# Local attention of a two-layer attention block on one Trainium2 core: elementwise products replaced by block matmuls with masks as contraction rows

## Chip, cores and metric

One core of a Trainium2 chip. The metric is device time in microseconds (us) of one execution; the page and the traces are of one profiled execution.

## What is computed

The input x has 16 images of 64 channels and 56 x 56 pixels, float32. Two residual layers follow each other:

```python
x = x + L0(_gn(x), ...)   # window attention: 7 x 7 windows, 16 channels a head
x = x + L1(_gn(x), w_out, b_out)
# L1, local attention, KSIZE 5, 8 heads of 8 channels:
patches = extract_patches(x)                        # 25 shifted copies, zero outside the image
p = patches.reshape(N, NHEADS, hdim, K2, H, W)
q = x.reshape(N, NHEADS, hdim, 1, H, W)
scores = (p * q).sum(axis=2, keepdims=True)
att = jax.nn.softmax(scores, axis=3)                # over the 25 shifts
out = (p * att).sum(axis=3).reshape(N, D, H, W)
out = jnp.einsum('ndhw,od->nohw', out, w_out) + b_out[None, :, None, None]
```

`_gn` normalises groups of two channels over the image. A pixel outside the image has score 0 and value 0, but it counts in the softmax's total.

## The kernel before, in words

Partitions hold two images by 64 channels; the 8 pairs of images are `BP`. There are three stages.

Stage 1, window attention (the functions up to L1162 on DVE, L1361 on PE): 64 units in a loop, each with four passes of scores (L1321), transposes (L1330) and weighing (L1346). It is the same in both kernels. After it, DVE and PE compute the second layer's group statistics; the last step of that is L1065.

Stage 2, local attention, L1186 to L1247 on DVE, L1419 to L1498 on PE. x1 is written to DRAM with a border of zeros (`widen_x1`, L583) and is read back in two layouts, one for scores and one for values. Then for each of the 8 heads j:

- Scores: 13 shifts of a half plane times 2 channel halves. A product of pixels and shifted pixels, 128 x 1568, is made on DVE for head 0 (L1194) and on POOL for the others (L799), with the square on ACT. PE adds the channels with the matrix `fold` (`sum_scores`, L1428 and L1432), and ACT copies the map twice, once mirrored (L965, L969).
- Softmax: DVE takes the maximum of 25 maps (L1203) and subtracts it (L1209), ACT takes exponentials (L988), PE adds the total (L1444 to L1461), DVE inverts it (L1227).
- Values: 25 shifts times 2 halves. ACT copies a weight map to PSUM (`place_weight`, L997), DVE multiplies it into shifted pixels (L1220), or POOL does (L810), and PE adds the products with the identity (`sum_values`, L1484), 16 matmuls of 32 x 32 tiles for each product. ACT copies the sum out (L1008), POOL scales it (L815), SP stores it in DRAM.

The order on all engines in stage 2 is written by a planner, `merge_orders` (L173), which simulates the steps with written costs. Tiles go round in rings of four (`ring`, `v_tiles`).

Stage 3: attention and x1 are loaded from DRAM, PE projects (L1507: 64 matmuls of 392 columns with 128 x 128 weights), DVE adds (L1255), SP stores.

## Time and profile before

| what | value |
|---|---|
| runs, median of 2 | 1743.34 us (1738.09 to 1748.59) |
| profiled execution, span from first to last instruction | 1743.6 us |
| PE busy | 1434.3 us, 82% |
| DVE busy | 1396.1 us, 80% |
| ACT busy | 1030.6 us, 59% |
| POOL busy | 1139.6 us, 65% |
| DMA | 152.35 MB, mean 87 GB/s |

The span and the median agree within 0.3 us, so a sum that is made in the profiled execution stands for the runs. Busy time is the union of an engine's instructions: where 16 matmuls run side by side in different tiles of the array, they count once. "PEld" are the weight loads, which lie beside the matmuls. "Idle before" is time that an engine spent without work ahead of a group, with what ended it.

### The profile page before, as it was taken

Reading aid. Unit: us, or ns where it says so; the run is one execution under the profiler, and the core shown is the slowest. Engines: PE = TensorE matmul, PEld = TensorE weight load, DVE = VectorE, ACT = ScalarE, POOL = GpSimd, SP = SyncE. Lnnn points to the kernel's source line nnn. Section 1 sums busy time; section 2 is a strip of 40 time slices with the busy share of each in tenths; the row PEclk is TensorE's granted clock in tenths of the full one; section 3 lists DMA queues with packets and bytes.
Section 4 is the critical chain, followed back from the end, with each engine's and each line's share of the span. In section 5 each row is a group of like instructions: output and inputs, shape, how many; then the busy total and the mean of one; then the engine's idle time right before and its main releaser. Section 6 shows DMA issues by size and latency. Waiting matters only on the chain.

```text
span 1743.6 us, 62829 instructions
## 1 busy us (share of the span) xinstructions
PE 1434.3 (82%) x26281; PEld 755.6 (43%) x26281; DVE 1396.1 (80%) x1964; ACT 1030.6 (59%) x1861; POOL 1139.6 (65%) x873
## 2 busy tenths in 40 slices
PE   4989999999999999974597888879797786966754
PEld 2656666666666666651132332323233232322332
DVE  4774777777777777778999999999989999995933
ACT  3554777777777777754564747667474766543300
POOL 5333555555555555530679999999999999985700
PEclk9775999999999999987699999999999999997978
DMA  8702011111104220215202324223232522126079
GB/s 330 301 11 52 18 34 39 28 46 24 50 17 100 21 55 18 55 33 141 52 20 59 98 52 122 52 73 91 58 79 51 122 52 71 39 67 244 22 309 388
DMA packets 106870, 152.35 MB, mean 87 GB/s; under 512 B 71362, under 2 KB 83650, under 8 KB 100034
## 3 DMA queue, kind: packets, MB, share of 16 engines
q1 hardware_dynamic: 106690, 149.67, 29.4%
q8 instruction: 147, 2.41, 0.6%
q14 instruction: 33, 0.27, 0.1%
HBM read 77.99 MB, written 65.20 MB: 82 GB/s over the span
## 4 chain that ended last, share of the span: by engine, by line
PE 44%; DVE 18%; POOL 16%; issue 13%; ACT 5%; SPq 1%; DMA 1%; DVEq 0%; POOLq 0%; ACTq 0%
POOL arena L799 11%; PE PS L1484 7%; PE PS L1321 7%; PE PS L1330 5%; PE PS L1346 5%; DVE arena L1111 4%; PE PS L1298 4%; POOL arena L810 4%; PE PS L1290 4%; DVE arena L1107 4%; PE PS L1507 3%; PE PS L1428 3%; PE PS L1309 2%; PE PS L1360 2%; ACT arena L988 2%
## 5 line engine op out<-in xcount | busy, mean ns | idle before, releaser
L1220 DVE TENSOR_TENSOR arena<-arena,PS 128x1568 f32<-128x1568 f32 x334 | 583.9, 1777 | 16.1 <-PE PS L1484 8.3
L799 POOL TENSOR_TENSOR arena<-arena 128x1568 f32<-128x1568 f32 x168 | 517.7, 3123 | 87.7 <-PE PS L1428 68.1
L765 POOL TENSOR_TENSOR arena<-arena,consts 128x196 f32<-128x196 f32 x512 | 294.3, 609 | 283.7 <-ACT arena L849 283.7
L1484 PE MATMUL PS<-arena,consts 32*32 32x392 f32 x12800 | 396.9, 512 | 78.3 <-DVE arena L1220 23.4
L997 ACT ACTIVATE PS<-arena 128x392 f32<-128x392 f32 x334 | 166.3, 501 | 255.8 <-DVE arena L1220 255.1
L1428 PE MATMUL PS<-arena,consts 128*32 128x392 f32 x1664 | 200.3, 554 | 83.2 <-POOL arena L799 42.1
L1107 DVE TENSOR_REDUCE arena<-PS 128x8 f32<-128x392 f32 x256 | 143.2, 559 | 144.7 <-PE PS L1321 143.2
L1484 PEld LDWEIGHTS PS<-arena,consts 32*32 32x32 f32 x12800 | 145.8, 104 | 246.0 <-issue 96.1
L874 ACT ACTIVATE arena<-PS 128x512 f32<-128x512 f32 x256 | 152.9, 597 | 161.0 <-PE PS L1330 157.2
L810 POOL TENSOR_TENSOR arena<-arena 128x1568 f32<-128x1568 f32 x66 | 202.7, 3081 | 29.4 <-ACT arena L937 20.7
L1330 PE MATMUL PS<-consts,arena 128*128 128x128 f32 x1024 | 177.9, 299 | 0.2
L1346 PE MATMUL PS<-arena 128*64 128x34 f32 x4096 | 176.8, 232 | 0.7 <-DVE arena L1124 0.7
L1321 PE MATMUL PS<-arena 64*64 64x196 f32 x2048 | 166.4, 397 | 1.8 <-POOL arena L765 1.1
L1346 PEld LDWEIGHTS PS<-arena 128*64 128x64 f32 x4096 | 147.5, 143 | 46.8 <-issue 46.0
L1111 DVE TENSOR_TENSOR arena<-PS,arena 128x392 f32<-128x392 f32 x256 | 145.4, 568 | 18.7
L867 ACT ACTIVATE arena<-arena 128x392 f32<-128x392 f32 x256 | 137.8, 538 | 33.1 <-DVE arena L1111 24.0
L772 POOL TENSOR_TENSOR arena<-arena 128x392 f32 (+1 forms) x64 | 78.4, 1225 | 109.3 <-DVE arena L1136 109.3
L1330 PEld LDWEIGHTS PS<-consts,arena 128*128 128x128 f32 x1024 | 113.9, 147 | 64.4 <-issue 52.2
L1428 PEld LDWEIGHTS PS<-arena,consts 128*32 128x32 f32 x1664 | 35.8, 112 | 219.7 <-issue 102.1
L928 ACT ACTIVATE arena<-arena,consts 128x504 f32<-128x504 f32 (+1 forms) x128 | 104.8, 856 | 14.6 <-DMA arena<-x_wide_dram 9.7
L862 ACT ACTIVATE arena<-PS 49x256 f32<-49x256 f32 x256 | 95.5, 373 | 24.6 <-PE PS L1309 23.1
L1203 DVE TENSOR_TENSOR PS<-arena,PS 128x392 f32<-128x392 f32 x192 | 108.1, 563 | 2.2
(109 smaller groups left out, 1724.2 us busy)
## 6 DMA issues: line engine op xcount, KB each, us to landing
arena<-x_wide_dram SPq DMA_DIRECT2D x32, 660.0 KB, 8.2
arena<-x_wide_dram SPq DMA_DIRECT2D x256, 67.5 KB, 2.0
x_wide_dram<-arena SPq DMA_DIRECT2D x12, 1125.0 KB
arena<-in_x_dram SPq DMA_DIRECT2D x8, 1568.0 KB, 14.5
x_wide_dram<-arena SPq DMA_DIRECT2D x64, 196.0 KB, 4.3
x_dram<-arena SPq DMA_DIRECT2D x8, 1568.0 KB, 7.5
attn_dram<-arena SPq DMA_DIRECT2D x256, 49.0 KB, 3.0
arena<-x_dram SPq DMA_DIRECT2D x8, 1568.0 KB, 19.0
```

The lines of the kernel that those rows point to most:

```text
L765: i = nc.gpsimd.tensor_tensor(k_bd[k][:, r], keys.unsqueeze(1).to_broadcast([P, HEADS_T, S]), head_mask.unsqueeze(2).to_broadcast([P, HEAD ...
L799: nc.gpsimd.tensor_tensor(tile, x_part, by, ALU.mult).then_inc(pool_tile, 1)
L810: nc.gpsimd.tensor_tensor(tile, *by, ALU.mult).then_inc(pool_tile, 1)
L997: nc.scalar.activation(PS[:, 2 + n % W_BANKS, 0:PIX], sc[j % 2][:, k, :], ACT.Copy).then_inc(weight_placed, 1)
L1107: nc.vector.tensor_reduce(by_tile(row_max[k % 2]), bank, AX_X, ALU.max).then_inc(max_done, 1)
L1111: nc.vector.tensor_tensor(probs[k].rearrange("p (j i) s -> p i j s", i=2)[:, :, :, 0:S], bank, by_tile(row_max[k % 2]).unsqueeze(3).to_bro ...
L1220: nc.vector.tensor_tensor(by_channel(v_tiles[n % V_RING]), shifted_values(half, k), over_channels(PS[:, 2 + n % W_BANKS, 0:PIX]), ALU.mult ...
L1321: mm = nc.tensor.matmul(dst, residue(qk_sb[up][b2], e, r)[rows], k_bd[k][rows, r], start=True, stop=True)
L1330: i = nc.tensor.transpose(PS[:, 7, j * P:(j + 1) * P], probs[k][:, 2 * j:2 * j + 2, :].rearrange("p h s -> p (h s)"), ident)
L1346: i = nc.tensor.matmul(PS[rows, 6, VW * j:VW * j + VN], probs_T[k % 2][:, j, rows], v_bd[up][e][:, b2 * 4 + j + 8 * r, 0:VN], start=True, ...
L1428: mm = nc.tensor.matmul(PS[g * GROUP:(g + 1) * GROUP, 0, above:above + PIX], fold, tile[:, g * PIX:(g + 1) * PIX], start=a == 0, stop=a == ...
L1484: mm = nc.tensor.matmul(PS[dst, 4 + i, 0:PIX], ident[src, src], tile[src, c * PIX:(c + 1) * PIX], start=done == 0, stop=done == NK - 1)
```

## The change

Stage 1 stays, instruction by instruction. Stages 2 and 3 are replaced.

The image is cut into blocks of 4 x 7 pixels. Their keys lie in a region of 8 x 11 pixels (88 keys). One matmul has the block as its stationary operand (8 channels of one head as rows, 28 pixels padded to 32 as columns) and the region as moving operand: 32 x 88 scores. 22 more contraction rows (8 to 29) hold masks: they add 0 to a score of a key within 5 x 5 of the pixel, and multiples of -65536 to the others. So the stationary operand has 30 rows, plus the 31st in the second pass.

The 64 channels of a pair of images make 4 sets `k` of 4 heads `r` (32 sets in all). A set has 7 strips `t` of 8 image rows; a strip has 16 blocks for each head, 4 quads `q` of 4 blocks `c`. All is one pipeline of steps `g`:

- First score pass, 10 steps ahead (`LEAD`): `for_max_quad` (PE, L1293) fills a PSUM bank with 4 x 88 scores for each of 128 rows (4 blocks x 32 pixels), `maxima` (DVE, L1079) reduces it. Once for each set PE turns the maxima (L1348), DVE places them negated as a row of pixels (L1092), and SP loads that row as contraction row 30 of the region (`load_max`, L466).
- Second score pass: `for_exp_quad` (L1310), the same matmuls with row 30, so the maximum is subtracted. ACT takes the exponential of the bank (L874). It is the weight with keys as columns and pixels as partitions.
- Values: `sum_strip` (PE, L1326 and L1340) contracts over the 128 partitions with pixels' values spread into a block diagonal by POOL (`spread_values`, L737), and with ones for the totals, and adds into maps of 8 x 18 pixels per block column pair. A matmul of zeros (L1326) clears the bank. ACT copies the maps (L886).
- Once for each set, in halves: `fold_totals` and `fold_sums` (L1367, L1377) add the maps to rows of pixels. The totals go to 128 x 112 through SP (L475), DVE inverts them (L1097), SP sends them through DRAM to all channels (L482, L488), DVE multiplies (L1105), SP gathers the set into `attn` (L498).
- For each pair of images: PE turns the values (L1392), projects (L1399), DVE adds (L1113), SP stores. That is the old stage 3, now inside the pipeline, with one `spare_bank` for turns, folds and projections.

Before unit 0 of stage 1 POOL builds the mask tables and clears three buffers (`local_attention_tables`, L604 to L669 of the new file), and SP lays them out.

The diff, cut to its core:

```diff
+SETS = 4 * BP
+HEADS_S = 4
+PART = P // HEADS_S
+BLOCK_H, BLOCK_W = 4, 7
+REGION_H, REGION_W = BLOCK_H + 4, BLOCK_W + 4
+KEYS = REGION_H * REGION_W
+BANDS = H // BLOCK_H
+STRIPS = BANDS // 2
+QUADS = 4 * STRIPS
+FILLS = HEADS_S * STRIPS
+COLS = 2 * BLOCK_W + 4
+MAP = REGION_H * COLS
+MAPS = HR * COLS
+LEAD = 10
+EXPAND = 4
+STEPS = SETS * STRIPS
+HALF = REGION_H * W
...
+def max_turned_at(g):
+    k, t = divmod(g, STRIPS)
+    return k + 1 if t == 4 and 0 <= k + 1 < SETS else None
...
+def folded_at(g):
+    k, t = divmod(g, STRIPS)
+    if t == 6 and 0 <= k - 1 < SETS:
+        return k - 1, 0
+    if t == 0 and 0 <= k - 2 < SETS:
+        return k - 2, 1
+    return None
...
-            def value_product(step):
-                _, j, half, k = step
-                pool.wait_ge(xv_ready[half], j + 1)
-                pool.wait_ge(lexp_done, SUB_PARTS * j + k // KS + 1)
-                room_in_ring(step)
-                tile = by_channel(ring[RING_AT[step] % S_RING][:, 0:CH * PIX])
-                by = shifted_values(half, k), over_channels(sc[j % 2][:, k, :])
-                if ALL_SHIFTS[k][1] == -1:
-                    by = by[::-1]
-                nc.gpsimd.tensor_tensor(tile, *by, ALU.mult).then_inc(pool_tile, 1)
...
+                for c in range(4):
+                    to = v_bd2[heads_of(c), 4 * t:4 * t + 4, :, c]
+                    i = nc.gpsimd.tensor_copy(to, v_T[heads_of(c), 4 * t:4 * t + 4, j * PART:(j + 1) * PART]
+                                              .rearrange("p n (r d) -> p n r d", d=HD))
+                i.then_inc(values_spread, 1)
...
-            def place_weight(n):
-                _, j, _, k = V_ORDER[n]
-                if k % KS == 0 or n == 0 or V_ORDER[n - 1][2] != V_ORDER[n][2]:
-                    act.wait_ge(lexp_done, SUB_PARTS * j + k // KS + 1)
-                if n >= W_BANKS:
-                    act.wait_ge(v_made, n + 1 - W_BANKS)
-                nc.scalar.activation(PS[:, 2 + n % W_BANKS, 0:PIX], sc[j % 2][:, k, :], ACT.Copy).then_inc(weight_placed, 1)
...
+            def exponentials_of_strip(k, t, i):
+                g, r = STRIPS * k + t, (i + 2) % HEADS_S
+                f = HEADS_S * g + i
+                act.wait_ge(for_exp, f + 1)
+                if i == 0 and g >= 2:
+                    act.wait_ge(strip_summed, g - 1)
+                nc.scalar.activation(w_keys[g % 2][r], PS[:, exp_banks[f % 3], 0:4 * KEYS], ACT.Exp).then_inc(exp_taken, 1)
...
+                for n in (t, t + 1)[:1 if t < STRIPS - 1 else 2]:
+                    cells = MAP if n < STRIPS else MAP // 2
+                    src = PS[:, sum_banks[n % 2], 0:2 * MAP].rearrange("p (m n) -> p m n", m=2)
+                    nc.scalar.activation(maps[:, k % 2::2 - k % 2, n * MAP:n * MAP + cells], src[:, :, 0:cells],
+                                         ACT.Copy).then_inc(sums_copied, 1)
...
-                nc.vector.tensor_tensor(by_channel(v_tiles[n % V_RING]), shifted_values(half, k),
-                                        over_channels(PS[:, 2 + n % W_BANKS, 0:PIX]), ALU.mult).then_inc(v_made, 1)
...
+            def maxima(k, t, r):
+                f = FILLS * k + HEADS_S * t + r
+                dve.wait_ge(for_max, f + 1)
+                if t == 0 and r == 0 and k >= 2:
+                    dve.wait_ge(max_turned, k - 1)
+                at = r * QUADS + 4 * t
+                nc.vector.tensor_reduce(m_T[k % 2][:, at:at + 4], PS[:, max_banks[f % 2], 0:4 * KEYS]
+                                        .rearrange("p (q n) -> p q n", q=4), AX_X, ALU.max).then_inc(max_taken, 1)
...
+            def normalise_sums(k, h):
+                dve.wait_ge(sum_folded, 2 * k + h + 1)
+                dve.wait_ge(inv_loaded, 16 * (k + 1))
+                rows = slice(0, PART * len(fold_halves(h)))
+                v = inv_wide[rows, h * HALF:(h + 1) * HALF]
+                nc.vector.tensor_tensor(v, PS[rows, spare_bank, 0:HALF], v, ALU.mult).then_inc(out_norm, 1)
...
-            def sum_scores(task):
...
-                        mm = nc.tensor.matmul(PS[dst, 4 + i, 0:PIX], ident[src, src], tile[src, c * PIX:(c + 1) * PIX],
-                                              start=done == 0, stop=done == NK - 1)
...
+            def for_max_quad(k, t, r, q):
+                f = FILLS * k + HEADS_S * t + r
+                if q == 0:
+                    if f >= 2:
+                        pe.wait_ge(max_taken, f - 1)
+                    if t == 0 and r == 0:
+                        pe.wait_ge(pixels_loaded[k % 3], 128 * (k // 3 + 1))
+                by, s = 2 * t + q // 2, q % 2
+                for c in range(4):
+                    n = by, 2 * c + s
+                    i = nc.tensor.matmul(PS[heads_of(c), max_banks[f % 2], q * KEYS:(q + 1) * KEYS]
+                                         .rearrange("p (h w) -> p h w", h=REGION_H),
+                                         block_pixels(k, r, n, MAX_ROW), region(k, r, n, MAX_ROW), start=True, stop=True)
+                if q == 3:
+                    i.then_inc(for_max, 1)
...
+                for c in range(4):
+                    n = by, 2 * c + s
+                    mm = nc.tensor.matmul(PS[heads_of(c), exp_banks[f % 3], q * KEYS:(q + 1) * KEYS]
+                                          .rearrange("p (h w) -> p h w", h=REGION_H),
+                                          block_pixels(k, r, n, MAX_ROW + 1), region(k, r, n, MAX_ROW + 1),
+                                          start=True, stop=True)
+                if q == 3:
+                    mm.then_inc(for_exp, 1)
...
+            def sum_strip(k, t):
+                g = STRIPS * k + t
+                pe.wait_ge(exp_taken, HEADS_S * (g + 1))
+                pe.wait_ge(values_spread, g + 1)
+                if g:
+                    pe.wait_ge(sums_copied, EVICTS * k + t)
+                for bank in (t, t + 1)[t > 0:]:
+                    for r in range(HEADS_S):
+                        nc.tensor.matmul(PS[heads_of(r), sum_banks[bank % 2], 0:2 * MAP], ident[0:PART, PART:2 * PART],
+                                         pick_heads[0:PART, 0:2 * MAP], start=True, stop=False)
+                pieces = [(t, s, 0, REGION_H, 0) for s in range(2)]
+                pieces += [(t, 2 + s, 0, BLOCK_H, BLOCK_H) for s in range(2)]
+                pieces += [(t + 1, 2 + s, BLOCK_H, BLOCK_H, 0) for s in range(2)]
+                for n, (bank, q, first, lines, to) in enumerate(pieces):
+                    s = q % 2
+                    for m in range(2):
+                        stop = m == 1 and (n == 3 or (n == 5 and t == STRIPS - 1))
+                        for r in range(HEADS_S):
+                            out_map = PS[heads_of(r), sum_banks[bank % 2], m * MAP:(m + 1) * MAP].rearrange(
+                                "p (h w) -> p h w", w=COLS)
+                            keys = w_keys[g % 2][r][:, q * KEYS:(q + 1) * KEYS].rearrange("p (h w) -> p h w", h=REGION_H)
+                            by = key_ones if m else v_bd2[:, 4 * t + q, r].rearrange("p c d -> p (c d)")
+                            i = nc.tensor.matmul(out_map[:, to:to + lines, BLOCK_W * s:BLOCK_W * s + REGION_W], by,
+                                                 keys[:, first:first + lines], start=False, stop=stop)
+                i.then_inc(strip_summed, 1)
...
+                for n, (c, first, last, start) in enumerate(pieces):
+                    at = first - (2 * BLOCK_W * c - 2)
+                    for w in fold_halves(h):
+                        lines = REGION_H * (2 * w + h) + 2
+                        src = maps[:, 2 if m else k % 2, lines * COLS:(lines + REGION_H) * COLS].rearrange("p (h w) -> p h w", w=COLS)
+                        dst = PS[heads_of(w), spare_bank, 0:HALF].rearrange("p (h w) -> p h w", w=W)
+                        i = nc.tensor.matmul(dst[:, :, first:last], pick[:, c * PART:(c + 1) * PART],
+                                             src[:, :, at:at + last - first], start=start, stop=n == len(pieces) - 1)
...
+                for n in range(2):
+                    for w in fold_halves(h):
+                        band = 4 * w + 2 * h + n
+                        nc.tensor.matmul(PS[heads_of(w), spare_bank, n * BLOCK_H * W:(n + 1) * BLOCK_H * W],
+                                         pick_heads[0:BAND_ROWS, band * PART:(band + 1) * PART], e_pad[k % 2][0:BAND_ROWS],
+                                         start=n == 0, stop=False)
...
+            for g in range(FIRST_STEP, LAST_STEP + 1):
+                k1, t1 = at_step(g + LEAD)
+                k2, t2 = at_step(g)
+                for r in range(HEADS_S):
+                    for q in range(4):
+                        if k1 is not None:
+                            for_max_quad(k1, t1, r, q)
+                        if k2 is not None:
+                            for_exp_quad(k2, t2, r, q)
+                    if r == 1:
+                        if g in VALUES_OF:
+                            await_spare(g, 0)
+                            turn_values(*VALUES_OF[g])
+                        elif g in OUTPUT_OF:
+                            await_spare(g, 0)
+                            project(*OUTPUT_OF[g])
+                        elif max_turned_at(g) is not None:
+                            await_spare(g, 0)
+                            turn_max(max_turned_at(g))
+                k, t = at_step(g - 1)
+                if k is not None:
+                    sum_strip(k, t)
+                if totals_at(g):
+                    await_spare(g, 1)
+                    fold_totals(*totals_at(g))
+                elif folded_at(g):
+                    await_spare(g, 1)
+                    fold_sums(*folded_at(g))
...
```

On PE, in the middle of stage 2, the order stood as follows (L1484 adds value products, L1428 and L1432 add score products, L1444 adds four maps for the total):

```order
L1428 MATMUL PS<-arena,consts 32x392 x4
L1484 MATMUL PS<-arena,consts 32x392 x64
L1428 MATMUL PS<-arena,consts 32x392 x4
L1484 MATMUL PS<-arena,consts 32x392 x32
L1428 MATMUL PS<-arena,consts 32x392 x4
L1432 MATMUL PS<-arena,consts 32x112 x4
L1484 MATMUL PS<-arena,consts 32x392 x16
```

In the changed kernel the last fill of a strip, the sums of the strip before and the first quad of the next strip stand so:

```order
L1293 MATMUL PS<-arena 32x88 [waits max_taken]
L1293 MATMUL PS<-arena 32x88 x3
L1310 MATMUL PS<-arena 32x88 [waits exp_taken]
L1310 MATMUL PS<-arena 32x88 x3
...
L1326 MATMUL PS<-consts 32x288 [waits sums_copied,values_spread,exp_taken]
L1326 MATMUL PS<-consts 32x288 x3
L1340 MATMUL PS<-arena 32x8x11 x4
L1340 MATMUL PS<-arena,consts 32x8x11 x4
...
L1340 MATMUL PS<-arena 32x4x11 x4
L1340 MATMUL PS<-arena,consts 32x4x11 x4
...
L1293 MATMUL PS<-arena 32x88 [waits pixels_loaded2,max_taken]
```

What was 16 matmuls of 392 columns for each product that another engine had made is now a sequence of matmuls of 88 and 44 columns, and the engines behind PE only read what it leaves in PSUM.

On DVE, before, the row of one head stood so: the end of the maximum (L1203), the subtraction (L1209), value products (L1220) with the inverse between them (L1227), then the next head's maximum:

```order
L1203 TENSOR_TENSOR PS<-arena,PS 128x392 x2
L1209 TENSOR_TENSOR arena<-arena,PS 128x1960 x5
L1220 TENSOR_TENSOR arena<-arena,PS 128x1568 x18
L1227 RECIPROCAL consts<-PS 128x392
L1220 TENSOR_TENSOR arena<-arena,PS 128x1568 x3
L1203 TENSOR_TENSOR PS<-arena,PS 128x392
```

And now (reductions of a bank, with the placing of maxima, the inverse, the normalisation and the output addition between them):

```order
L1079 TENSOR_REDUCE arena<-PS 128x4 x4
L1092 COPY arena<-PS 56x4x4x7 x2
L1097 RECIPROCAL arena<-arena 128x112
L1079 TENSOR_REDUCE arena<-PS 128x4 x10
L1105 TENSOR_TENSOR arena<-PS,arena 128x448
L1079 TENSOR_REDUCE arena<-PS 128x4 x4
L1105 TENSOR_TENSOR arena<-PS,arena 96x448
L1079 TENSOR_REDUCE arena<-PS 128x4 x10
L1113 SCALAR_TENSOR_TENSOR arena<-PS,consts,arena 128x448
```

DVE no longer writes tiles for PE; it reads PE's banks and frees them.

Counted over the whole program, the new local stage has 43,704 matmuls on PE: 28,672 of 88 columns for the two score passes, 10,752 of 88 or 44 for sums and totals, 1,024 clearing ones of 288, 2,464 of up to 144 columns and 448 of 224 for the folds, 224 of 128 (value turns), 64 of 128 (maximum turns), 56 of 448 (projections). Before, stages 2 and 3 had 8,648.

## Rows read from the trace of the kernel before

**Rows 1.** The page: busy time (share) xinstructions; granted TensorE clock in 40 slices

```profile
PE 1434.3 (82%) x26281; PEld 755.6 (43%) x26281; DVE 1396.1 (80%) x1964; ACT 1030.6 (59%) x1861; POOL 1139.6 (65%) x873
...
PEclk9775999999999999987699999999999999997978
```

**Rows 2.** Busy time by stage: stretch, its length, busy of each engine (xinstructions), clock, DMA

```profile
0.00:783.60 783.60, 699.42 (x8976) 473.80 (x8976) 542.28 (x1325) 530.98 (x1034) 382.45 (x624) 0.94 0.23 68
783.60:1655.20 871.60, 689.90 (x17177) 256.33 (x17177) 822.45 (x623) 499.64 (x828) 757.19 (x249) 0.93 0.31 78
1655.20:1743.60 88.40, 45.00 (x128) 25.48 (x128) 31.36 (x17) 0.00 (x0) 0.00 (x0) 0.77 0.85 345
```

**Rows 3.** Waits from 860 to 1655 us: who for whom, total us, times, longest

```profile
ACT PS L997 <- DVE arena L1220: 255.1, 218, 11.9
...
PEld PS L1484 <- DVE arena L1220: 86.6, 116, 5.0
...
PEld PS L1428 <- POOL arena L799: 56.3, 36, 4.6
```

**Rows 4.** Groups by form: count | busy us, mean ns of one | idle before

```profile
L1220 DVE TENSOR_TENSOR arena<-arena,PS 128x1568 f32<-128x1568 f32 x334 | 583.9, 1777 | 16.1 <-PE PS L1484 8.3 <-ACT PS L997 5.9
L799 POOL TENSOR_TENSOR arena<-arena 128x1568 f32<-128x1568 f32 x168 | 517.7, 3123 | 87.7 <-PE PS L1428 68.1 <-PE PS L1432 19.6
...
L1346 PE MATMUL PS<-arena 128*64 128x34 f32 x4096 | 176.8, 232 | 0.7 <-DVE arena L1124 0.7
...
L1107 DVE TENSOR_REDUCE arena<-PS 128x8 f32<-128x392 f32 x256 | 143.2, 559 | 144.7 <-PE PS L1321 143.2 <-DVE consts L1073 0.3
...
L965 ACT ACTIVATE arena<-PS 128x392 f32<-128x392 f32 x104 | 50.7, 487 | 73.5 <-PE PS L1432 51.8 <-PE PS L1428 21.7
...
L1432 PE MATMUL PS<-arena,consts 128*32 128x56 f32 x640 | 24.2, 222 | 0.0
```

**Rows 5.** The projections: their group, and weight loads in order of time (start, us)

```profile
L1507 PE MATMUL PS<-arena,consts 128*128 128x392 f32 x128 | 45.0, 516 | 21.5 <-DMA arena<-attn_dram 21.5
...
1677.39 0.34 PEld L1507 LDWEIGHTS PS<-arena,consts 128*128 128x128 f32 x1 [0.32 <-issue]
1678.04 0.34 PEld L1507 LDWEIGHTS PS<-arena,consts 128*128 128x128 f32 x1 [0.32 <-issue]
1678.70 0.34 PEld L1507 LDWEIGHTS PS<-arena,consts 128*128 128x128 f32 x1 [0.32 <-issue]
```

**Rows 6.** PE in order of time in the middle of stage 2: start, us

```profile
1101.27 0.29 PE L1432 MATMUL PS<-arena,consts 128*32 128x56 f32 x8
1101.50 2.81 PE L1484 MATMUL PS<-arena,consts 32*32 32x392 f32 x96
1104.24 0.87 PE L1428 MATMUL PS<-arena,consts 128*32 128x392 f32 x8
1105.04 0.95 PE L1484 MATMUL PS<-arena,consts 32*32 32x392 f32 x32
1105.92 0.87 PE L1428 MATMUL PS<-arena,consts 128*32 128x392 f32 x8
```

**Rows 7.** PE in order of time near the end of stage 1

```profile
770.94 0.66 PE L1346 MATMUL PS<-arena 128*64 128x34 f32 x16
```

**Rows 8.** POOL in order of time at the head of the program

```profile
9.53 1.97 POOL L748 MEMSET arena<- 128x2250 f32 x1
...
24.84 4.50 POOL L765 TENSOR_TENSOR arena<-arena,consts 128x196 f32<-128x196 f32 x8 [10.20 <-ACT arena L849]
```

**Rows 9.** PE in order of time, from the statistics to the first local matmul

```profile
783.61 0.38 PE L1410 MATMUL PS<-consts 128*16 128x128 f32 x1 [0.94 <-DVE consts L1065]
...
798.44 1.53 PE L1428 MATMUL PS<-arena,consts 128*32 128x392 f32 x8 [13.38 <-DVE arena L1194]
```

**Rows 10.** The page: the instruction queue; one load's size and time to landing

```profile
q8 instruction: 147, 2.41, 0.6%
...
arena<-x_wide_dram SPq DMA_DIRECT2D x256, 67.5 KB, 2.0
```

1258 lines of the change are left out of this document (539 added, 719 removed).

## The prediction

> **What bounds the kernel now.** I read the page's busy line and slices first, then the same kernel cut at the two places where its work changes, then the waits and groups of the middle stretch, then single stretches of TensorE. [rows 1] show no engine full over the whole span (PE 82%, DVE 80%), so the average says little. [rows 2] cut it: 783.6 us of window attention, 871.6 us of local attention, 88.4 us of output projection. In the middle stretch DVE is busy 822 of 871.6 us, POOL 757, PE 690. [rows 3] say what the middle waits for: ACT, with time to spare, waits 255 us for DVE, and the long waits of PE are for DVE and POOL tiles. [rows 4] name the work: 334 value products on DVE at 1.78 us and 168 score products on POOL at 3.12 us. So the elementwise products bound the local attention. PE takes part but is not its limit; its granted clock there is 0.93, so the fuller PE of the new stage should see the full clock (the higher of the two levels, 2.4 GHz), at which the prices below were read. The change touches that stretch and the last one: 1743.6 - 783.6 = 960 us.
>
> How many run side by side? In [rows 6] one L1484 product (16 matmuls, 32 instructions, 16 different 32x32 tiles) takes 0.95 us and three take 2.81, so 0.93 for each further one against 0.655 of pure streaming: all 16 tiles do run together, with 0.275 us lost per 16 matmuls. L1428 (four tiles of 128x32) takes 0.87 for 8 instructions: four together. A change of the tile form costs: L1428 to L1484 starts 0.80 apart, L1484 to L1428 0.88, against 0.655 of streaming, so 0.15 to 0.23 us each; I take 0.17.
>
> **The change, part by part.**
>
> Local attention moves to PE. Per strip the new order has four fills, each of four quads, each quad four L1293 matmuls (for the maximum) and four L1310 matmuls (for the exponent). The stationary operand is 30 or 31 rows by 32 pixels, 88 columns move. All quads of a fill use the same 8 tiles: row group r for the one pass, r + 2 for the other. So the streaming bound of a fill is 4 x 0.147 = 0.59 us, 2.35 us per strip for 128 matmuls. The upper bound puts the 0.275 us of [rows 6] on every 16 matmuls: 2.35 + 8 x 0.275 = 4.55. Which between? One matmul lives about 0.03 (weights) + 0.073 (first pass) + 0.24 (second, by the 222 ns mean of a 56-column pass, whose streaming is 47 [rows 4]) = 0.34 us, and 16 in flight is the most that the rows show. That gives 0.34 / 16 = 21 ns per matmul, 2.75 us per strip. Then the maximum has two banks only. A fill f+2 waits for the reduction of fill f: 0.64 us into it for its last maximum matmul, 0.34 to finish, about 0.52 for the reduction (L1107 takes 0.559 for 392 elements [rows 4], here 352), 0.17 for two hops. So fill f+2 enters 1.67 us after f: fills enter at 0, 0.69, 1.67 and 2.36 (the pause for the sums clears the first two), and the last is in at 3.05. I take 3.1 us, the value nearest to the lifetime of a short pass in these rows.
>
> Sums of a strip (after the scores, L1326 and L1340): four zeroing matmuls of 288 columns on four tiles, 0.48 us; then per column tile 4 matmuls of 88 and 8 of 44 columns, 4 x 0.147 + 8 x 0.073 = 1.17 us, on four tiles of 128x32. With changes of form into it, out of it and the last completion 3 x 0.17: a strip costs 3.1 + 0.48 + 1.17 + 0.45 = **5.2 us** on PE. There are 32 sets x 7 = 224 strips.
>
> What else runs on PE, streaming plus 0.4 for two changes of form where it breaks into another form: 64 total folds (448 + 544 columns: 0.75 + 0.91 + 0.4 = 2.05) 131 us; 64 sum folds in the form of the sums (0.91) 58; 56 value turns (4 x 0.214 + 0.4 = 1.25) 70; 56 projections (0.75 + 0.4) 64; 32 maximum turns (0.43 + 0.4) 27. Together 350 us, of which 268 stream.
>
> Other engines, to see whether they hide behind this. DVE: 4 x 0.52 = 2.1 us per strip plus some 0.5 us. ACT: four exponentials of 352 elements at about 0.47 (L965 takes 0.487 for 392 from PSUM [rows 4]) plus one copy of 288 elements: 2.3 us. POOL: four copies of 128 elements per strip. All lie under 5.2 us of PE, so they cost nothing, save that a DVE normalisation between two reductions delays the next fill: 64 x 0.3 = 20 us. The DMAs per set (pixels, blocks, maxima, inverse) lie beside 7 x 5.2 = 36 us; issue to landing of the 67.5 KB loads of before was 2.0 us [rows 10]. If that cover failed, a wait of 2 us per set would be 64 us in all.
>
> The removed work (all products, the widened copy of x1, its loads and the separate 88.4 us at the end) saves the 960 us whole. The projection comes back inside, as counted.
>
> Ahead of unit 0 POOL now builds the mask tables, two memsets of 3,600 elements (L748: 2,250 in 1.97 us, so 3.1 each [rows 8]) and some 50 small steps at 0.2 to 0.7: about 20 us from 15 on, so they end near 35 while POOL before began its first keys at 24.84 [rows 8]. I take 10 us; bounds 0 and 15.
>
> **The sum.** End of window attention 783.6 + 10 = 794. Scale, blocks and first loads 13 (before, PE's first local matmul also came at 798.4, 15 us after [rows 9]). The first 10 steps hold only maxima, 2.5 each: 25. 214 full steps x 5.2 = 1113. The last 10 strips without maxima, 4.6 each: 46. Second zeroing in the first strip of a set 32 x 0.48 = 15. Other PE work 350. DVE 20. Tail (last fold, two trips of the inverse through memory, gather, seven projections in turn, last store) 30. Sum 2406. The page's span is 1743.6 and the median of the runs 1743.3, so no correction: **2406 us**, slower by 38%.
>
> **A rule against the trace.** [rows 6] have eight 56-column instructions of L1432 in 0.29 us at a mean of 222 ns each, so they start some 10 ns apart. The Trainium skill (TensorE: Matmul & The Clock Gate, "Back-to-back issue gap") says instead that a small matmul never starts within about 25 ns of the last. By that rule 87,408 local instructions take 2185 us and the total would be near 3.1 ms. The 10 ns of the trace speak against it.
>
> **The rivals.**
>
> A, a floor per instruction. L1346 has 16 short instructions in 0.66 us: (0.66 - 0.23) / 15 = 28.5 ns each [rows 4, 7]. If the new stream of small matmuls ran so, 43,704 x 2 x 28.5 ns = 2491 us, total about 806 + 2491 + 55 = 3350. For it: each new matmul is small. Against it: L1346 loads 64 columns on only two tiles, and L1432 shows 10 ns.
>
> B, the supply of instructions. 147 packets of 16 KB came on the instruction queue, 0.6% of 16 engines' span, 1.14 us each [rows 10]. The new local stage has 174,816 PE instructions of 64 bytes: 683 packets. At 1.14 us that is 779 us and hidden behind 1600. From 2.35 us per packet on it decides; at 3 us the local stage takes 2050 and the total is 2900.
>
> C, the array full, the other side: not slower. If the score passes of neighbouring fills used all 16 tiles (28,672 x 0.147 / 16 = 263 us), the zeroing and all changes of form hid behind them, the sums (263) and other work (268) only streamed, the total would be 806 + 263 + 263 + 268 + 55 = 1655, faster by 5%. It decides from (1743 - 806 - 64 - 320) / 224 = 2.5 us per strip downwards. Against it: quads of a fill come back to the same 8 tiles, and three identical products in [rows 6] never came nearer than 0.93 to 0.655.
>
> D, fills that don't overlap: 0.275 us per 16 matmuls as in [rows 6], 4.55 instead of 3.1 per strip: 2406 + 224 x 1.45 = 2731.
>
> **How the numbers follow.** Forecast 0.66, D 0.17, A 0.06, B 0.06, C 0.03, nothing of these 0.02 (about no change). The range takes the streaming bound of the scores and half the form changes below (2406 - 168 - 40 - 82 = about 2120) and D with a tail of misjudged waits above: 2120 to 2800. About 2% is what a measurement can tell from no change; slower by more than that 0.95, within 0.02, faster 0.03.
>
> **What would show it.** Right: PE above 90% busy from 810 us on, DVE near 40 to 50% there, a strip every 5.2 us, the sums of a strip near 1.7, POOL nearly idle. Waits of L1293 for the reductions small. Wrong: strips of 2.5 to 3 us (C), a gap of PE with the releaser "issue" between quads (A or B; with B the instruction queue's packets come back to back), or PE waiting for ACT or a DMA at the head of each set.

## The result, and the profile after

The changed kernel takes **3655.15 us** (3651.81 to 3658.50), the kernel before 1743.34 in the same comparison: a ratio of 2.102, 95% interval 2.083 to 2.120. The forecast was 2406, range 2120 to 2800. The sign was right; 1249 us were missing.

The page of the changed kernel: span, busy time (share) xinstructions, the slices of PE and of the granted clock, and the queues.

```profile
span 3656.8 us, 205318 instructions
...
PE 2971.9 (81%) x96384; PEld 2243.5 (61%) x96384; DVE 1116.7 (31%) x2437; ACT 1087.5 (30%) x2338; POOL 785.9 (21%) x1738
...
PE   6899999958877887878778887888788878877886
...
PEclk9899999975666666666676566657656766776676
...
q8 instruction: 696, 11.40, 1.3%
...
PE 76%; issue 15%; DVE 6%; ACT 1%; POOL 1%; DMA 1%; SPq 0%; DVEq 0%; POOLq 0%; ACTq 0%
```

15% of the chain is "issue", time for which the profile shows nothing that was waited for. The instruction queue carried 696 packets, where [rows 10] have 147.

By stage, columns as in [rows 2] (stretch, length, busy of PE, PEld, DVE, ACT, POOL, then clock, DMA share, GB/s):

```profile
0.00:783.60 783.60, 689.29 (x8976) 468.39 (x8976) 543.64 (x1325) 532.49 (x1034) 399.19 (x673) 0.98 0.12 45
...
860.00:3600.00 2740.00, 2212.55 (x85990) 1725.21 (x85982) 550.22 (x1072) 549.47 (x1294) 376.25 (x1042) 0.66 0.20 38
```

Stage 1 is as it was. The other engines are busy for about a fifth of the long stretch or less. They wait for PE (waits: engine, line, for whom: us, times, longest), and PE's weight loads, which go ahead of its passes, wait for "issue":

```profile
DVE arena L1079 <- PE PS L1293: 2177.1, 861, 22.8
ACT arena L874 <- PE PS L1310: 2173.9, 847, 14.4
...
PEld PS L1293 <- issue: 318.5, 307, 22.3
...
PEld PS L1340 <- issue: 255.5, 287, 8.6
PEld PS L1310 <- issue: 217.6, 144, 9.1
```

The groups by form that answer to the terms of the forecast:

```profile
L1310 PE MATMUL PS<-arena 31*32 31x88 f32 x28672 | 1013.2, 299 | 182.5 <-issue 181.4
L1293 PE MATMUL PS<-arena 30*32 30x88 f32 x28672 | 1001.8, 302 | 209.0 <-issue 182.5 <-DMA arena<-arena 22.2 <-DVE arena L1079 4.0
...
L1326 PE MATMUL PS<-consts 32*32 32x288 f32 x2048 | 292.4, 628 | 25.1 <-issue 24.9
```

The counts are those of the forecast, and no other engine stands among the large waits of PE: from the first local matmul on, its waits for ACT, DVE and loads add up to about 100 us, the largest 27.4 us (for ACT, L1399). By the forecast's count the stage has 174,816 instructions of 64 bytes for TensorE, 683 packets or *pages* of 256. With the forecast's own 806 us ahead of the stage and 55 behind it, 3655 - 861 = 2794 us, 4.09 us a page.

### The profile page after: what moved, and what is told of

The parts are those of the page before. It is cut to its first block, busy times and chain, and to the rows that moved or that the text cites. A ratio compares the mean times of both kernels' runs of the same rounds, so it can differ in the third digit from the quotient of the medians.

```text
span 3656.8 us, 205318 instructions
## 1 busy us (share of the span) xinstructions
PE 2971.9 (81%) x96384; PEld 2243.5 (61%) x96384; DVE 1116.7 (31%) x2437; ACT 1087.5 (30%) x2338; POOL 785.9 (21%) x1738
## 4 chain that ended last, share of the span: by engine, by line
PE 76%; issue 15%; DVE 6%; ACT 1%; POOL 1%; DMA 1%; SPq 0%; DVEq 0%; POOLq 0%; ACTq 0%
PE PS L1293 17%; PE PS L1340 15%; PE PS L1310 11%; PE PS L1326 6%; PE PS L1367 5%; PE PS L1193 3%; PE PS L1392 3%; PE PS L1377 2%; PE PS L1399 2%; PE PS L1202 2%; PE PS L1218 2%; DVE arena L1011 2%; PE PS L1170 2%; DVE arena L1007 2%; PE PS L1162 2%
## 5 line engine op out<-in xcount | busy, mean ns | idle before, releaser
L1293 PE MATMUL PS<-arena 30*32 30x88 f32 x28672 | 1001.8, 302 | 209.0 <-issue 182.5
L1310 PE MATMUL PS<-arena 31*32 31x88 f32 x28672 | 1013.2, 299 | 182.5 <-issue 181.4
L1079 DVE TENSOR_REDUCE arena<-PS 128x4 f32<-128x352 f32 x896 | 469.9, 524 | 2179.1 <-PE PS L1293 2177.1
L874 ACT ACTIVATE arena<-PS 128x352 f32<-128x352 f32 x896 | 414.6, 464 | 2176.5 <-PE PS L1310 2173.9
L1293 PEld LDWEIGHTS PS<-arena 30*32 30x32 f32 x28672 | 814.4, 128 | 354.7 <-issue 318.5
L1310 PEld LDWEIGHTS PS<-arena 31*32 31x32 f32 x28672 | 775.0, 126 | 219.5 <-issue 217.6
L737 POOL COPY arena<-arena 32x128 f32<-32x128 f32 x896 | 257.0, 287 | 1786.9 <-PE PS L1340 1703.8
L1340 PE MATMUL PS<-arena 128*32 128x44 f32 (+1 forms) x10752 | 508.7, 295 | 28.7 <-issue 28.7
L1340 PEld LDWEIGHTS PS<-arena 128*32 128x32 f32 x10752 | 381.6, 163 | 220.6 <-issue 220.3
L1340 PE MATMUL PS<-arena,consts 128*32 128x44 f32 (+1 forms) x10752 | 489.8, 294 | 28.8 <-issue 28.7
L1340 PEld LDWEIGHTS PS<-arena,consts 128*32 128x32 f32 x10752 | 396.8, 168 | 35.6 <-issue 35.2
L1326 PE MATMUL PS<-consts 32*32 32x288 f32 x2048 | 292.4, 628 | 25.1 <-issue 24.9
L1367 PE MATMUL PS<-arena,consts 128*32 128x128 f32 (+4 forms) x4928 | 201.6, 303 | 28.4 <-issue 18.9
L1367 PEld LDWEIGHTS PS<-arena,consts 128*32 128x32 f32 x4928 | 160.2, 139 | 63.6 <-issue 46.9
L1007 DVE TENSOR_REDUCE arena<-PS 128x8 f32<-128x392 f32 x256 | 143.1, 559 | 146.9 <-PE PS L1193 145.7
```

Of the source, the lines that this page charges most:

```text
L737: i = nc.gpsimd.tensor_copy(to, v_T[heads_of(c), 4 * t:4 * t + 4, j * PART:(j + 1) * PART] .rearrange("p n (r d) -> p n r d", d=HD))
L874: nc.scalar.activation(w_keys[g % 2][r], PS[:, exp_banks[f % 3], 0:4 * KEYS], ACT.Exp).then_inc(exp_taken, 1)
L1079: nc.vector.tensor_reduce(m_T[k % 2][:, at:at + 4], PS[:, max_banks[f % 2], 0:4 * KEYS] .rearrange("p (q n) -> p q n", q=4), AX_X, ALU.max ...
L1293: i = nc.tensor.matmul(PS[heads_of(c), max_banks[f % 2], q * KEYS:(q + 1) * KEYS] .rearrange("p (h w) -> p h w", h=REGION_H), block_pixels ...
L1310: mm = nc.tensor.matmul(PS[heads_of(c), exp_banks[f % 3], q * KEYS:(q + 1) * KEYS] .rearrange("p (h w) -> p h w", h=REGION_H), block_pixel ...
L1326: nc.tensor.matmul(PS[heads_of(r), sum_banks[bank % 2], 0:2 * MAP], ident[0:PART, PART:2 * PART], pick_heads[0:PART, 0:2 * MAP], start=Tru ...
```

## The experiments

Four theories. **S**: unrolled code comes in pages of 256 instructions, one every so many microseconds, whatever is in them. **T**: the columns streamed decide. **F**: the changes of tile form decide. **A**: the forecast's rival, a fixed 28.5 ns for each pass with its load. The expectations use the letter F for two things: in those of m1_supply, e_half_columns, e_no_value_sums and e_small_loads it is the floor for each load and pass, which the text here calls A; in the later ones it is the changes of form. D is the forecast's. In straight code A and S give nearly the same number, 128 x 28.5 ns = 3.65 us for 256 instructions, so only code that isn't straight can part them. Eleven kernels were run; for those that vary the changed kernel the ratio is to the kernel before, with its 95% interval. The kernel before itself took 1734 to 1743 us in these comparisons, so a difference of some tens of us between two variants means little.

### TensorE's stream alone

m1_supply runs seven stretches on TensorE alone, each closed by a small VectorE memset. A fill is 32 matmuls (128 instructions) like those of L1293 and L1310; a strip is four fills, the zeroing and the 48 sums, 720 instructions.

```diff
+            for f in range(40):
+                i = long_scores(f)
...
+            with pe.Fori(0, 20) as n:
+                for f in range(4):
+                    i = loop_scores(f)
```

> No attention is computed, the output is x; seven stretches of matmuls alone, no waits inside, a DVE memset after each. (1) 40 fills of 32 score matmuls of 88 columns written out, (2) the same with 44 columns, (3) the fills in a hardware loop of 4 fills, 20 rounds, (4) loop of 16 fills, 5 rounds, (5) loop of 24 fills, 4 rounds, (6) a whole strip (4 fills and its sums) in a loop, 24 rounds, (7) 12 strips written out. Theory S (instructions come in pages of 256, one ahead, 3.3 to 3.8 us each): (1) 20 pages, 66 to 76 us, and (2) the same; (3) and (4) free of it, 0.6 to 0.8 us a fill, so 48 to 64 us for 80 fills; (7) 34 pages, 112 to 130 us, against (6) about 5 us a strip, 120 us for 24. Theory F (a floor of 28 ns for each load and pass): 1.8 us a fill in all of (1) to (5), 144 us for (3) and (4), 10 us a strip in (6) and (7). Theory T (the forecast, streaming and 16 in flight): 0.7 us a fill everywhere, 28 us for (1), less for (2), 60 us for (7).

Its stretches in order (stretch, length, busy of PE, PEld, DVE, POOL; granted clock, DMA share, GB/s):

```profile
65.50:138.80 73.30, 50.23 (x2560) 43.83 (x2560) 0.00 (x0) 0.00 (x0) 1.00 0.02 4
138.90:212.00 73.10, 34.18 (x2560) 30.53 (x2560) 0.01 (x1) 0.00 (x0) 1.00 0.02 4
212.10:308.20 96.10, 92.90 (x5122) 89.84 (x5122) 0.00 (x0) 0.00 (x0) 1.00 0.00 1
308.30:471.60 163.30, 103.21 (x5122) 89.06 (x5122) 0.00 (x0) 0.00 (x0) 1.00 0.02 4
471.70:665.10 193.40, 122.93 (x6146) 106.78 (x6146) 0.02 (x1) 0.00 (x0) 1.00 0.02 4
665.30:792.10 126.80, 123.20 (x8642) 107.86 (x8642) 0.00 (x0) 0.00 (x0) 1.00 0.00 0
792.30:916.60 124.30, 94.00 (x4320) 76.49 (x4320) 0.00 (x0) 0.00 (x0) 0.63 0.02 4
```

- 40 fills unrolled, 88 columns: 73.3 us, 1.83 a fill. With 44 columns: 73.1. T falls.
- 80 fills as a loop of four (512 instructions): 96.1, 1.20 a fill. That is far from the unrolled 1.83, but S had expected 0.6 to 0.8 (48 to 64 us), which is the streaming at the full level; the 1.20 fit the streaming at the lower level, 2 x 0.59 = 1.18 by the forecast's price (on the recorded clock see the last section). S had also expected the loop of 16 fills to be free of the supply, and it isn't: loops of 16 and of 24 fills (2,048 and 3,072 instructions) are fetched again on each turn, at 2.04 and 2.01 a fill, and the DMA column shows traffic (0.02, where the loop of four has 0.00). The instruction queue of the whole kernel carried 173 packets. The stretches that are fetched throughout hold 20 + 20 + 40 + 48 + 34 = 162 pages; the loops of four fills and of the strip would add 40 and 68 if they were fetched on each turn, and 2 and 3 if once; 11 are left for them and the rest.
- 24 strips as a loop of one (720 instructions): 126.8, 5.28 a strip. 12 strips unrolled: 124.3, 10.4 a strip. Same instructions, twice the time.

The first stretch in order of time shows the mechanism (start, us, group, idle before it):

```profile
98.19 2.50 PE L73 MATMUL PS<-data 30*32 30x88 f32 x128 [1.50 <-issue]
101.65 2.51 PE L73 MATMUL PS<-data 30*32 30x88 f32 x128 [0.95 <-issue]
105.10 2.51 PE L73 MATMUL PS<-data 30*32 30x88 f32 x128 [0.95 <-issue]
```

128 passes and their 128 loads are 256 instructions, one page. PE runs them in 2.5 us and stands 0.95 until the next page is there: 3.45 here, 73.3 / 20 = 3.67 over the stretch. And the strip that is held in a loop, once round:

```profile
701.17 3.06 PE L93 MATMUL PS<-data 30*32 30x88 f32 x252
...
704.66 1.44 PE L123 MATMUL PS<-data 128*32 128x88 f32 x96
...
706.19 3.06 PE L93 MATMUL PS<-data 30*32 30x88 f32 x252
```

One strip every 706.19 - 701.17 = 5.02 us at the full granted clock, the scores in 3.06. That is near the forecast's 5.2 and 3.1 for the work, changes of form included, so F can't be what doubles it. A falls too: 28.5 ns for each of 360 passes would be 10.3 a strip here as well. The agreement of 3.06 with 3.1 is in part luck: the forecast's 3.1 holds a wait for the reductions (two banks of maxima), and this loop has none; without it the forecast had 2.75.

m2_sizes asks three more things: how long a loop can be and not be fetched again, what the 0.93 us of the 16-tile product in [rows 6] is, and what half the instructions do.

```diff
+            for n in range(64):
+                i = product_out()
...
+            with pe.Fori(0, 32) as n:
+                for f in range(2):
+                    product_loop()
```

> A kernel of TensorE stretches alone, after the same data traffic as m1_supply has at its head (it computes nothing of the reference). Theory S (unrolled code is brought in pages of 256 instructions, one every 3.45 to 3.8 us; a loop that fits is not brought again). Theory X (the 0.93 us of a product of 16 392-column matmuls is lost in the array itself). Stretch 1, 64 products of 16 tiles unrolled, 4,096 instructions, 16 pages: S 16 x 3.45 to 3.8 = 55 to 61 us; X 64 x 0.93 = 60. Stretch 2, the same 64 products in a loop of 2 products: S 64 x 0.655 = 42 us at the higher clock level (84 at the lower), X 60 again. Stretches 3, 4 and 5, the score fills of 88 columns in loops of 8, 10 and 12 fills (1,024, 1,280 and 1,536 instructions; 80, 80 and 84 fills): S, where a loop still fits, 58 us (higher level) to 96 us (lower), where it doesn't, 2.0 us a fill: 160 to 170. The loop of 720 instructions fitted and that of 2,048 didn't, so I expect 1,024 to fit and 1,536 not to. Stretch 6, 80 fills in bf16 unrolled, one load and one pass for each matmul, 5,120 instructions, 20 pages: S 20 x 3.67 = 73 us, half of the 147 of fp32; a cost per matmul, whatever its instructions, would give 147.

```profile
65.20:123.10 57.90, 57.66 (x2048) 38.00 (x2048) 0.00 (x0) 0.00 (x0) 1.00 0.02 4
123.30:178.00 54.70, 54.64 (x2050) 37.49 (x2050) 0.00 (x0) 0.00 (x0) 1.00 0.00 0
178.30:271.20 92.90, 88.98 (x5122) 87.75 (x5122) 0.00 (x0) 0.00 (x0) 0.52 0.00 1
271.40:365.30 93.90, 90.36 (x5122) 88.06 (x5122) 0.00 (x0) 0.00 (x0) 0.50 0.00 1
365.50:464.80 99.30, 94.93 (x5378) 92.33 (x5378) 0.00 (x0) 0.00 (x0) 0.50 0.00 1
465.00:535.30 70.30, 27.22 (x2560) 23.48 (x2560) 0.00 (x0) 0.00 (x0) 0.50 0.02 5
```

- Loops of 1,024, 1,280 and 1,536 instructions are all kept: 1.16, 1.17 and 1.18 us a fill at a granted 0.50 to 0.52, DMA share 0. The whole kernel moved 51 packets; its two unrolled stretches are 36 of them, and the four loops fetched on each turn would be 138. 15 are left, what the four bodies are once. My 1,536 was a miss. The end lies between 1,536 and 2,048.
- bf16 (last stretch): one load and one pass for each matmul, 80 fills in 70.3 us, 0.88 a fill against 1.83. In pages it is 70.3 / 20 = 3.5 us. The cost hangs on the instructions, not on the matmuls.
- The 392-column product: unrolled 57.9 / 64 = 0.905 us, in a loop 54.7 / 64 = 0.855. S had expected 0.655 of pure streaming and X 0.93, so both missed. The weight loads of the loop show where a part of it may be:

```profile
124.83 1.45 PEld L73 LDWEIGHTS PS<-data 32*32 32x32 f32 x64 [0.26 <-issue]
126.52 1.48 PEld L73 LDWEIGHTS PS<-data 32*32 32x32 f32 x64 [0.23 <-issue]
128.26 1.46 PEld L73 LDWEIGHTS PS<-data 32*32 32x32 f32 x64 [0.26 <-issue]
```

The loads of two products take 1.45 to 1.48, 0.74 each, and about 0.24 passes until the next turn's first load. That 0.74 is the array and 0.24 the turn of the loop is an estimate from these rows; the passes themselves show no gap (PE is busy 54.64 of 54.70 us). Four products are exactly one page (4 x 64 = 256 instructions): unrolled, 57.9 / 16 = 3.62 us. The 0.93 of [rows 6] gives 4 x 0.93 = 3.7 us, the same number, but the same cause isn't shown for it. Around those rows (1100 to 1107 us of the kernel before) PE had 208 passes and 192 loads in 7 us, a page every 4.5 us, slower than the supply.

### Parts of the changed kernel

**Half the columns.** Both score passes stream 44 columns instead of 88, and DVE and ACT take 44 (half of the keys are left out).

```diff
-   block_pixels(k, r, n, MAX_ROW), region(k, r, n, MAX_ROW), start=True, stop=True)
+   block_pixels(k, r, n, MAX_ROW), region(k, r, n, MAX_ROW)[:, 0:REGION_H // 2], start=True, stop=True)
```

> Both score passes take only the first 4 of the 8 lines of a region (44 columns instead of 88), DVE and ACT read only those; the number of instructions is the same. Left out: half of the keys. S: within 2% of 3655 us. T, and every theory in which the array's streaming bounds: 1.17 us less a strip, 263 us less (7%). F: no change.

Measured 3649.69 us (ratio 2.096, 2.068 to 2.123): no change. T is refuted in the kernel too.

**Fewer instructions.** The value sums are left out (`for m in (1,)` in `sum_strip`); only the totals remain: 5,376 matmuls, 84 pages.

```diff
-                    for m in range(2):
+                    for m in (1,):
```

> The matmuls that add the values (half of L1340, 5,376 matmuls, 21,504 PE instructions, 84 pages) are left out; totals stay. S: 84 pages at the mean of 4.08 us, 343 us less, 3310 us. T: 0.59 us less a strip, 131 us less. F: 10,752 x 28.5 ns = 306 us less.

Measured 3475.56 (1.996, 1.971 to 2.020): 180 us less, 2.14 for each page taken away. S had expected 3310, A 3349 (its 306 us less), T 3524: a miss for all, between S and T. By itself this run decides nothing, and why these pages gave so little stays open.

**bf16 scores.** The upper halves of the fp32 words of pixels and blocks are read as bf16: the same 28,672 score matmuls and columns, half the instructions.

```diff
-            return b_buf[k % 3][r * PART:r * PART + rows, at:at + PART]
+            high = b_buf[k % 3].bitcast(BF16).rearrange("p (n two) -> p n two", two=2)
+            return high[r * PART:r * PART + rows, at:at + PART, 1]
```

> The changed kernel with the operands of the score matmuls read as bf16 (the upper half of each fp32 word), so that each of the 28,672 runs as one load and one pass: 57,344 instructions fewer, 224 pages. Theory S (supply, 3.8 to 4.1 us a page): 3655 - 224 x 3.8 to 4.1 = 2740 to 2800 us. Theory D of the forecast (fills don't overlap, 0.275 us lost per 16 matmuls, the streaming halved): 3655 less at most 224 x 1.18 = 264, about 3390. Theory F (the changes of tile form cost the time): they stay, also 3390 or more.

**Both in bf16.** The same for the operands of the sums (L1340).

```diff
+                            by = by.bitcast(BF16).rearrange("p (n two) -> p n two", two=2)[:, :, 1]
```

> As e_bf16_scores, and the operands of the 10,752 sum matmuls as bf16 too: 21,504 instructions fewer again, 84 pages. Theory S: another 84 x 3.8 = 320 us less if these pages are bound by their supply, about half of it (150 to 200) if, as e_no_value_sums has it, a part of them is bound by their own execution; in all 2420 to 2650 us. Theories D and F: about 3200.

**More instructions, the same columns.** Each matmul of the exponent's pass is cut into two of 44 columns.

```diff
+                    for half in range(2):
...
+                                              block_pixels(k, r, n, MAX_ROW + 1), region(k, r, n, MAX_ROW + 1)[:, 4 * half:4 * half + 4],
```

> The changed kernel with each matmul of the exponent's pass cut into two of 44 columns: the same result and the same columns streamed, 14,336 matmuls and 57,344 instructions more, 224 pages. Theory S: 3655 + 224 x 3.4 to 4.1 = 4420 to 4570 us. Theory T (columns streamed decide) and theory F (changes of form): no change, 3655 to 3700. Theory A (28.5 ns for each load and pass): 28,672 x 28.5 ns = 817 us more, 4470, as S; it falls by the loops of m1_supply alone.

The instruction queue of the three pages, in this order (packets, MB, share):

```profile
q8 instruction: 472, 7.73, 1.2%
```

```profile
q8 instruction: 388, 6.36, 1.1%
```

```profile
q8 instruction: 920, 15.07, 1.4%
```

The packets move by exactly the pages counted (696 - 224, - 84, + 224), and the time with them:

| kernel | packets | us | ratio to before | us for each page changed |
|---|---|---|---|---|
| bf16 scores | 472 | 2873.80 | 1.655 (1.639 to 1.670) | (3655.15 - 2873.80) / 224 = 3.49 |
| both in bf16 | 388 | 2625.95 | 1.512 (1.500 to 1.524) | (2873.80 - 2625.95) / 84 = 2.95 |
| split exponent pass | 920 | 4521.56 | 2.604 (2.582 to 2.625) | (4521.56 - 3655.15) / 224 = 3.87 |

D of the forecast wanted 3390 where 2874 came, and T and F wanted no change where 866 us were added. S has all three right in sign and nearly in size. So has A, since 28.5 ns for 28,672 passes are 817 us and for 10,752 passes 306: these three runs can't part the two, and A falls by the loops alone. Between 472 and 920 packets the slope is (4521.56 - 2873.80) / 448 = 3.68 us a page, which is the supply's own interval; above 3.68 a page the stages of these two and of the changed kernel have 324, 323 and 281 us. With both in bf16 the time lies in the range expected (2420 to 2650). bf16_scores missed its range of 2740 to 2800 by 74 us: the stage doesn't get back the whole 4.09 a page, so part of the 4.09 doesn't come and go with the pages.

### What the rest of the 4.09 is

Unrolled code alone takes 3.6 to 3.7 us a page. Three runs and one more kernel ask where 0.4 x 683 = 270 to 300 us come from.

**Small loads.** From the fourth set on, the loads of pixels and blocks carry one row or block instead of the whole (their results are left out); same instructions.

```diff
+                    n = PLANE if k < 3 else ROW
+                    sp.dma_start(a_buf[k % 3][r * PART:r * PART + HD, 0:n], xp[rows, 0:n]).then_inc(pixels_loaded[k % 3], 16)
```

> From the fourth set on, the loads of pixels and blocks for each set carry one line or 32 elements for each partition instead of all (27 MB less is moved; later sets use stale pixels). Same instructions. S with pages that also queue behind data: pages of a stretch with much data took 5.7 us against 3.8 without, 83 such pages, a part of them beside these loads: 30 to 100 us less. T and F: no change.

Measured 3604.22 (2.069, 2.039 to 2.100): 51 us less, inside the 30 to 100 that were expected, but the interval overlaps that of the changed kernel (2.083 to 2.120), so by itself it shows no change.

**Short passes.** Zeroing, sums, folds and projections stream far fewer columns; same instructions, same changes of form.

```diff
-                                                 keys[:, first:first + lines], start=False, stop=stop)
+                                                 keys[:, first:first + 1], start=False, stop=stop)
```

> The changed kernel with the same instructions and shorter passes everywhere but in the scores: zeroing 36 columns for 288, sums 11 for 88 and 44, folds of two lines for eight, the band matmul of the totals 112 for 224, projections 56 for 448 (the results of these parts are left out; the reciprocal of the totals is a constant and three banks are filled once at the head). 696 pages as before. The stage took 2793 us for 684 pages, 4.08 each, while unrolled code alone took 3.5 to 3.7. Theory S1 (the rest is execution: pages of sums, zeroing and folds last longer than a supply interval, above all at the lower clock level): 684 x 3.5 to 3.7 = 2395 to 2530, in all 3260 to 3390 us. Theory S2 (pages come slower beside the data transfers, whatever they hold): no change, 3600 to 3655 us. Theory F (changes of tile form): they all stay, no change either.

Measured 3659.16 (2.110, 2.090 to 2.129): no change, and my favourite explanation gone. PE's busy time went from 2971.9 to 2677.7 us and nothing came of it:

```profile
PE 2677.7 (73%) x96384; PEld 2176.3 (59%) x96384; DVE 1101.8 (30%) x2440; ACT 1089.2 (30%) x2338; POOL 785.7 (21%) x1738
...
PEclk9899999975555555555555555555555555555555
```

The granted clock was at its lower level for the whole stage (0.5) and the time didn't move. The streaming of the longer passes doesn't bound the changed kernel; a loss by the clock that just made up for the shorter passes isn't excluded by this run, but e_half_columns had 0.687 over the span and the same time too. The changes of form stayed, so F as a part of the rest isn't touched by this run.

**Few bytes.** Nearly all transfers of the local stage carry a row each; same instructions, waits and issues.

```diff
-                sp.dma_start(inv_wide, src).then_inc(inv_loaded, 16)
+                sp.dma_start(inv_wide[:, 0:W] if k else inv_wide, src).then_inc(inv_loaded, 16)
```

> The changed kernel with the same instructions, waits and issues of transfers, and nearly no bytes in those of the local stage: pixels and blocks of a set as in e_small_loads, and the raw images, the maxima, the inverse, the gather of the attention, x1 and the stores of the middle images cut to a row each (the output of these parts is left out). 696 pages. e_short_passes left the stage at 4.1 us a page, so execution isn't the rest. Theory S2 (data transfers hold the pages back): 684 x 3.5 to 3.7 + 861 = 3260 to 3390 us. Theory S3 (the pages themselves take 4.1 us in this stage, for instance because waits at their heads delay the request of the next): 3570 to 3620, little below e_small_loads.

Measured 3502.86 (2.011, 1.994 to 2.027): 152 us less, clear of noise, (3502.86 - 861) / 683 = 3.87 a page. About half of what S2 expected (3260 to 3390), and below what S3 did (3570 to 3620): neither had it. The waits of PE for loads were hardly touched, since the changed kernel had few (22.2 us before the first local matmul and 4.7 later, 22.2 and 4.5 here). In the trace of the changed kernel one such collision shows. Around 1908 us SP issues the load of x1 for a pair of images, and PE's next instructions are late:

```profile
1898.42 0.27 PE L1310 MATMUL PS<-arena 31*32 31x88 f32 x3 [0.96 <-issue]
...
1906.35 0.27 PE L1310 MATMUL PS<-arena 31*32 31x88 f32 x3 [1.29 <-issue]
...
1917.49 0.36 PE L1310 MATMUL PS<-arena 31*32 31x88 f32 x3 [8.73 <-issue]
```

```profile
1907.80:1917.40 9.60, 0.96 (x51) 0.64 (x34) 1.44 (x3) 0.77 (x2) 0.00 (x0) 0.50 0.88 103
```

The 16 DMA engines are 88% busy in that stretch and PE stands for 8.73 us, waiting for nothing that the profile shows. That the next page came behind the data is the reading of this, not a row. With few bytes (L1299, L1346 and L1316 are there what L1293, L1340 and L1310 are in the changed kernel) the longest such wait of the last two groups is 2.5 us, where it was 8.6 and 9.1; the 22.3 at the head of the stage both have:

```profile
PEld PS L1299 <- issue: 293.3, 316, 22.3
PEld PS L1346 <- issue: 228.6, 278, 2.3
PEld PS L1316 <- issue: 172.2, 136, 2.5
```

**The supply in company.** m3_company has six stretches of 10,240 unrolled instructions.

```diff
+            for section, form, count in ((1, 0, 50), (2, 1, 20), (3, 2, 200)):
+                sp.wait_ge(done, section)
```

> A kernel of TensorE stretches alone (it computes nothing of the reference). Every stretch has 10,240 unrolled instructions, 40 pages; 147 us at 3.67 a page. Stretch 1: 80 score fills alone: 140 to 150 us. Stretch 2: the same beside copies of eight rows of 14.4 KB on SP's queue, two in flight all the time: S2 expects 10 to 50% more, S3 the same. Stretch 3: beside loads of 64 x 56 lines of 224 bytes: S2 the same or more yet, S3 no change. Stretch 4: beside copies of 4 lines of 56 bytes, one after the other: near stretch 1 for both. Stretch 5: alone, with a change between 128x32 and 30x32 tiles every 16 matmuls: 160 changes; theory F 147 + 160 x 0.17 = 174 or more, theory S 147. Stretch 6: alone, and after every fourth fill (two pages) a wait for VectorE, 20 round trips of about 0.5 us: S3 at most +10 to +20 us, if a pause always delays the next page, 0 if a page that is already under way goes on coming.

```profile
66.00:211.70 145.70, 99.86 (x5111) 87.03 (x5091) 0.00 (x0) 0.00 (x0) 1.00 0.02 4
211.80:367.80 156.00, 100.67 (x5120) 87.52 (x5120) 0.00 (x0) 0.00 (x0) 1.00 0.36 41
367.90:555.20 187.30, 100.68 (x5120) 87.53 (x5120) 0.00 (x1) 0.00 (x0) 1.00 0.78 89
555.30:700.90 145.60, 100.67 (x5120) 87.52 (x5120) 0.00 (x0) 0.00 (x0) 1.00 0.02 5
701.00:867.10 166.10, 165.95 (x5120) 137.60 (x5120) 0.01 (x1) 0.00 (x0) 1.00 0.02 4
867.20:1011.20 144.00, 108.99 (x5122) 89.93 (x5122) 1.18 (x20) 0.00 (x0) 1.00 0.02 4
```

Alone 145.7 us (3.64 a page). Beside 50 copies of eight 14.4 KB rows +10 us (7%, under the 10 to 50% that S2 expected); beside 20 loads of 3,584 lines of 224 bytes +42 us (29%), 2.1 us for each of these loads; beside tiny copies and with 20 round trips to VectorE nothing. The fifth stretch can't answer for F: PE is busy 165.95 of its 166.1 us, so its own work, changes of form included, was longer than the supply. It was badly made. It does show that pages can take more than the supply's interval, 166.1 / 40 = 4.15 us each.

So some 150 of the some 300 us come from the bytes of the transfers, most likely in the way of the pages. The other 150 (3.87 against 3.64) stay open. Candidates that weren't separated: the waits of PE for ACT, DVE and loads (about 100 us in both traces), and pages whose own execution is longer, with several changes of form. The pages of the sums belong here: taking them away gave only 2.14 and 2.95 us each, and short passes in them nothing. No run shows why.

## Why the prediction was wrong, point by point

**The step that failed** is rival B's price and what hung on it: "At 1.14 us that is 779 us and hidden behind 1600." 1.14 is the time of one packet in transit, 0.6% of 16 engines' span over 147 packets. It is no interval, and the packets don't follow each other at that distance. In a stretch of unrolled code alone one came every 3.45 to 3.68 us, in the kernel every 4.09. With the count of the forecast that is 683 x 3.64 = 2486 us of supply alone, where the forecast had 779 hidden behind 1600. B's own threshold of 2.35 us a packet is passed by far. The mechanism stood in the text, with the right count, and got 0.06; I took the smallest bound there was for the interval. The trace of before had at most a hint: the products of [rows 6] at 0.93 each come to 3.7 us for 256 instructions. I read their 0.275 us over the streaming as lost in the array and priced rival D with them. In m2_sizes 0.20 of them stay in a loop too (0.855 a product) and 0.05 more come in unrolled code (0.905), so most of that reading isn't refuted.

The Trainium skill (Runtime: NRT & Kernel Launch, "Instruction fetch mechanics") has the 16 KB blocks of 256 instructions, fetched while the current block is executed. This case agrees with it on that (one page more or less for each 256 instructions, 472 and 920 packets). It goes on that crossing a block is mostly hidden. Here it isn't: PE waits 0.95 us at each page in m1_supply.

**"A strip costs 5.2 us."** Near for the work alone: 5.02 in the loop, scores 3.06 for my 3.1, the sums 1.44 for 1.17. That the scores agree so well is in part luck: the loop has no wait for reductions, and without one my figure was 2.75. The kernel has 2794 / 224 = 12.5 us a strip, other work included, where the forecast had (2406 - 861) / 224 = 6.9.

**"1.67 ns per column for both passes."** The right size for the full level, by a reading that is wrong twice. The weight loads of [rows 5], 0.655 us apart, lie in a stretch at a granted 0.50 (1676.5 to 1681 us of the kernel before: 7 passes, 8 loads), so each belongs to one pass, not to one projection, and not at the full level. At a granted 1.00 (1690 to 1697.5 us) 24 passes took 7.5 us, 0.31 each or 0.63 a projection. The two slips cancel. At the lower level the price is twice as high, and a fill streams in 1.18 us and not in 0.59.

**The lifetime of a short pass, the two banks of maxima, the changes of form, D's 0.275.** All sized something that lay under the supply. D falls by the loop, too: 3.06 us for the scores of a strip, where it had 4.55. DVE's reduction is 524 ns for my 520, ACT's exponential 464 for 470, and nearly all their waiting is for PE, as forecast.

**"The fuller PE should see the full clock."** Wrong: 0.66 over 860 to 3600 us, after 0.98 in stage 1. PE stood at page boundaries over and over, and the clock went up and down. No run shows a cost of it: e_short_passes and e_half_columns had it lower (0.603 and 0.687 over the span, for 0.720) at the same time.

**"The 10 ns of the trace speak against it."** The eight instructions of L1432 in 0.29 us were a burst, presumably out of a page already there. A burst says what the array takes, not what keeps coming. The rule's estimate of near 3.1 ms was nearer than mine, and for unrolled code 3.64 us for 128 loads with their passes is 28 ns each; but as a rule on TensorE it fails in a loop, where the same fills at the same form run at 3.06 / 256 = 12 ns.

**"I take 10 us" for the tables; start 13.** The tables cost nothing visible: the last statistics matmul before the stage starts at 780.4 us, where [rows 9] have 783.6. The first local matmul came at 803.2 for my 807. After 256 passes, two pages, PE then stood 11.28 us for the next instructions:

```profile
803.18 8.15 PE L1293 MATMUL PS<-arena 30*32 30x88 f32 x256 [22.20 <-DMA arena<-arena]
822.60 2.02 PE L1293 MATMUL PS<-arena 30*32 30x88 f32 x64 [11.28 <-issue]
```

**DMAs "lie beside".** Their landing did; their traffic didn't. It cost some 150 us, most likely through the pages, a path the forecast didn't have.

**Range and chances.** 2800 as the upper end came from D. B at its measured price gives 806 + 683 x 3.64 + 55 = 3347, and with the transfers 3500. A had 3350 in the forecast, the same number from a cause that the loops rule out. "Slower" at 0.95 was right, since every cause named led there but one; the cause that I held the likeliest isn't the one that set the time.

## What to carry to other kernels

Count the instructions of the unrolled code of TensorE (the one engine that was measured here), divide by 256, and give each page some 3.6 us where nothing else uses the DMA engines and 3.9 to 4.7 beside heavy traffic (156.0 / 40 and 187.3 / 40 in m3_company). That is 14 ns an instruction and 57 ns for an fp32 matmul, which is two loads and two passes: work smaller than that is bound by its code, not by the array, and fewer columns buy nothing. What helps is fewer instructions for the same work (bf16 scores gave 781 us here) or a loop whose body is kept, which ran the same strip in half the time. No run here put the local stage itself in such a loop. When a profile shows an engine neither full nor waiting for anyone ("issue"), look at how many packets the instruction queue moved and divide the stretch by them.

## What the runs showed of the hardware

- Unrolled TensorE code comes at 3.45 to 3.68 us for 256 instructions, with nothing else on the core's DMA engines; at 44 or 88 columns, fp32 or bf16, nearly the same (73.1, 73.3 and 70.3 us for 20 pages).
- A loop of 512 to 1,536 instructions isn't fetched again (DMA share 0, and 1.16 to 1.20 us a fill); loops of 2,048 and 3,072 are fetched in full each time round, at 4.0 to 4.1 us a page (163.3 / 40, 193.4 / 48), dearer than straight code. Between two turns of a loop of 128 instructions the weight loads pause for about 0.24 us.
- Beside transfers unrolled code comes slower: 145.7 us became 156.0 beside 5.8 MB in rows of 14.4 KB (DMA share 0.36) and 187.3 beside 16.1 MB in lines of 224 bytes (0.78). Bytes and form changed together, so which of them counts isn't shown. In the kernel one wait beside a share of 0.88 was 8.73 us.
- A wait of half a microsecond for another engine after every second page costs nothing (144.0 us with 20 of them, 145.7 without): the page seems to come meanwhile.
- The granted clock and the passes don't always tell the same. In m1_supply the loop of fills is recorded at 1.00, and in m2_sizes loops of the same fills at 0.50 to 0.52; both take 1.16 to 1.20 us a fill, and the passes last 346 and 345 ns:

```profile
L103 PE MATMUL PS<-data 30*32 30x88 f32 x5120 | 102.6, 346 | 60.2 <-issue 60.0 <-DVE mark L46 0.3
```

```profile
L92 PE MATMUL PS<-data 30*32 30x88 f32 x5120 | 89.8, 345 | 3.8 <-issue 3.5 <-DVE mark L47 0.3
```

  The first of these is the loop of 16 fills in a stretch recorded at 1.00; in the loop of four, also at 1.00, the mean is 345 ns too. Yet in the loop of the strip, at 1.00 again, the same pass lasts 251 ns. A clock read from one column is better checked against how long a known pass takes.
